# Gate and up products moved between the routing steps of a gated cross-attention and mixture-of-experts layer

## The chip, the cores and the metric

One core of a Trainium2 chip runs the whole layer in one program. The metric is the time of one execution on the device in microseconds (us), the median of several runs. The engines are PE (TensorE), DVE (VectorE), ACT (ScalarE), POOL (GpSimd) and SP (SyncE, which only issues transfers here). Each runs its own instructions in the order in which they are written, and waits on semaphores for the others.

## The reference

Inputs are x and ctx (4 batches of 512 tokens of 256 values), two gates g and the weights. All is float32.

```
x = x + tanh(g_xattn) * xattn(layernorm(x), ctx)      # 16 heads of 16, bias on q, k, v and output
h = layernorm(x)                                      # "h2" in the kernel
logits = h @ w_router;  top 2 of 8 experts, softmax over the two
moe    = sum over the two of score * (silu(h @ fc1[e][:, :256]) * (h @ fc1[e][:, 256:])) @ fc2[e]
shared = (silu(h @ gate_w) * (h @ up_w)) @ down_w     # gate_w, up_w: 256 x 512, down_w: 512 x 256
x = x + tanh(g_ffn) * (moe + shared)
```

## The kernel before

**Three stages.** First q, k, v and the attention of the 16 groups (4 batches of 4 groups of 4 heads). Last the slot stage: tokens stand sorted by expert in a DRAM tensor `slot_x`, 39 slots of 128 rows are loaded, multiplied with their expert's weights and scattered to `token_y`; behind it the shared products of batches 2 and 3 and the combination of everything. Between the two lies the stretch that the change touches, some 60 us long.

**What lies between attention and slots.** For each batch b the kernel transposes the attention's output (`ctx_transpose`), multiplies it with Wo (`out_projection`), adds it to x (`residual`, DVE), takes mean and variance (`statistics`, DVE), the reciprocal root of the variance (`rstd_second`, POOL), normalises (`normalised`, DVE), transposes (`h2_transpose`, copied out of PSUM by `h2t_first` on ACT and `h2t_second` on DVE), and multiplies with the router weights (`router`). DVE copies the logits (`logits`), picks two experts (`choose`), PE counts how many earlier tokens chose the same expert (`rank`), and DVE works out the row in `slot_x` (`place`). POOL then sends 8 indirect transfers per batch to that place (`scatter`, one per tile of 128 tokens and choice). Batches 0 to 2 have most of this behind them, or amid the last attention groups, when attention ends; batch 3 has it all ahead.

When all four batches are placed, PE sums the counts (`count`), DVE makes the table of slots (`tabulate`), SP clears the 8 ends of the experts' rows (line 355) and, when these and all 32 scatters have landed, loads the first three slots (line 362). PE transposes the first slot (`transpose_rows`, line 1321) and the slot stage begins.

**The filler.** The shared products of batches 0 and 1 need nothing but `H2T` of those batches and stand in the same stretch: `gate_up(b, c)` on PE (8 matmuls with 512 columns each), `silu(b, c)` on ACT, `hidden(b, c)` on DVE, for c from 0 to 3, then `down(b)` on PE (32 matmuls) and `shared_out(b, h)` on DVE.

**What sets the order.** It is written out by hand, once for each engine. Semaphore counts rise in that order, so the lists must fit together. PSUM has 8 banks. The routing steps take banks 3, 4 and 5 in turn, in the order of the list `USERS` (line 237), and each waits until the third step before it has been read (`bank_free`, line 1115). `gate_up` takes banks 0 and 1, or 2 and 6, or, for odd c of batch 1, banks 2 and 3; the first of these therefore waits for the logits of all batches (line 1250). It also waits until `hidden` has read the pair before the last (line 1255). `rstd_second(B - 1)` stands on POOL behind the 8 scatters of batch 0.

Of the kernel before, what the change touches and what calls it, by code (L numbers as in the profile page):

```python
# [15 lines left out]
def flamingo_layer(nc, x, ctxT, g_xattn, g_ffn, WqT, bq, WkT, bk, WvT, bv, WoT, bo,  # L16
                   w_router, fc1_w, fc2_w, gate_w, up_w, down_w, out):
    B, S, D = x.shape
# [4 lines left out]
    TB = S // P  # L23
# [5 lines left out]
    IC = ISH // P  # L29
# [26 lines left out]
    with ExitStack() as stack:  # L56
# [335 lines left out]
        def _(pool):  # L392
# [50 lines left out]
            def rstd_second(b):  # L443
                pool.wait_ge(ln_ve, B + b + 1)
                sl = slice(b * TB, (b + 1) * TB)
                nc.gpsimd.tensor_tensor(rstd[:, sl], var_eps[:, sl], minus_half[:, sl], ALU.pow).then_inc(ln_rstd, 1)  # L446

            def scatter(b):
                pool.wait_ge(tokens_in, 2)
                pool.wait_ge(placed, b + 1)  # L450
                for t in range(b * TB, (b + 1) * TB):
                    for k in range(2):
                        nc.gpsimd.indirect_dma_start(slot_x, bass.IndirectOffsetOnAxis(ap=pos[:, t, k:k + 1], axis=0),  # L453
                                                     CH[:, t, :], None).then_inc(scattered, 16)
# [5 lines left out]
            for b in range(B - 1):  # L460
                rstd_second(b)
            scatter(0)
            rstd_second(B - 1)
            for b in range(1, B):
                scatter(b)

            for j in range(SLOTS):
# [7 lines left out]
        def _(act):  # L475
# [70 lines left out]
            def ctt_first(b):  # L546
                act.wait_ge(ct_t, 2 * b + 1)
                if b >= 2:
                    act.wait_ge(wo_done, 2 * (b - 1))
                nc.scalar.copy(ctt(b, 0), PS[:, bank("ctx_t", b, 0), :]).then_inc(ctt_ready[0], 1)  # L550

            def h2t_first(b):
                act.wait_ge(h2_t, 2 * b + 1)
                nc.scalar.copy(H2T[:, 0, b * S:(b + 1) * S], PS[:, bank("h2_t", b, 0), :]).then_inc(h2t_ready[0], 1)
# [21 lines left out]
            def silu(b, c):  # L576
                n = IC * b + c
                act.wait_ge(gu_done, n + 1)
                if n >= 2:
                    act.wait_ge(hs_ready, n - 1)  # L580
                nc.scalar.activation(SG[:, n % 2, :], PS[:, gu_bank(n, 0), :], ACT.Silu).then_inc(silu_ready, 1)  # L581

            h2t_first(1)
            ctt_first(3)
            silu(0, 0)
            h2t_first(2)
            silu(0, 1)
            h2t_first(3)
            silu(0, 2)
            silu(0, 3)  # L590
            for b in range(1, BE):
                for c in range(IC):
                    silu(b, c)
                if b == 1:

                    act.wait_ge(gap_ready, 1)
                    nc.scalar.activation(sc[:, 1, :], sc[:, 0, :], ACT.Exp).then_inc(exp_sc, 1)
# [28 lines left out]
        def _(dve):  # L626
# [120 lines left out]
            def residual(b):  # L747
                dve.wait_ge(x_biased, TB * (b + 1))
                for h in range(2):
                    dve.wait_ge(wo_done, 2 * b + h + 1)  # L750
                    tt = slice(b * TB + 2 * h, b * TB + 2 * h + 2)
                    nc.vector.scalar_tensor_tensor(out=X[:, tt, :], in0=PS[:, bank("wo", b, h), :].rearrange("p (t d) -> p t d", t=2),
                                                   scalar=tg[:, 0:1], in1=X[:, tt, :], op0=ALU.mult, op1=ALU.add)\
                        .then_inc(x1_ready, 1)
# [5 lines left out]
            def h2t_second(b):  # L760
                dve.wait_ge(h2_t, 2 * b + 2)
                dve.wait_ge(st_done, G * TB * (GROUPS - 1 + b // 2))
                nc.vector.tensor_copy(H2T[:, 1, b * S:(b + 1) * S], PS[:, bank("h2_t", b, 1), :]).then_inc(h2t_ready[1], 1)

            def logits(b):
                dve.wait_ge(lg_done, b + 1)
                nc.vector.tensor_copy(LG[:, b * TB:(b + 1) * TB, :],
                                      PS[:, bank("router", b), 0:TB * E].rearrange("p (t e) -> p t e", t=TB)).then_inc(lg_ready, 1)


            def hidden(b, c):
                n = IC * b + c
                dve.wait_ge(silu_ready, n + 1)
                if b >= 2:
                    dve.wait_ge(down_done, 2 * (b - 1))
                nc.vector.tensor_tensor(HS[:, b % 2, c, :], SG[:, n % 2, :], PS[:, gu_bank(n, 1), :], ALU.mult)\  # L776
                    .then_inc(hs_ready, 1)

            def shared_out(b, h):
                dve.wait_ge(down_done, 2 * b + h + 1)  # L780
                tt = slice(b * TB + 2 * h, b * TB + 2 * h + 2)
                nc.vector.scalar_tensor_tensor(out=X[:, tt, :], in0=PS[:, 6 + h, :].rearrange("p (t d) -> p t d", t=2),
                                               scalar=tg[:, 1:2], in1=X[:, tt, :], op0=ALU.mult, op1=ALU.add)\
                    .then_inc(base_ready, 1)
# [34 lines left out]
            def place(b):  # L819
                sl = slice(b * TB, (b + 1) * TB)  # L820
                dve.wait_ge(ranked, b + 1)
                step(nc.vector.tensor_tensor(RK[:, :, :], PS[:, bank("rank", b), 0:TB * E].rearrange("p (t e) -> p t e", t=TB),
                                             ecap[:, :].unsqueeze(1).to_broadcast([P, TB, E]), ALU.add))
                step(nc.vector.tensor_tensor(PM[:, sl, :, :], OH[:, sl, :, :],
                                             RK[:, :, :].unsqueeze(2).to_broadcast([P, TB, 2, E]), ALU.mult))
                step(nc.vector.tensor_reduce(posf[:, sl, :], PM[:, sl, :, :], AX.X, ALU.add))
                nc.vector.tensor_copy(pos[:, sl, :], posf[:, sl, :]).then_inc(placed, 1)
                dve.wait_ge(placed, b + 1)
# [47 lines left out]
            def normalised(b):  # L876
                normalise(b, B, lambda t: CH[:, b * TB + t, 0:D], h2_ready)
# [20 lines left out]
            denominators(GROUPS - 1)  # L898
            head_out(GROUPS - 1)
            normalised(2)  # L900
            logits(1)
            choose(1)
            ctt_second(3)
            hidden(0, 0)
            place(1)
            residual(3)
            statistics(3)
            h2t_second(2)
            normalised(3)
            hidden(0, 1)  # L910
            logits(2)
            h2t_second(3)
            choose(2)
            hidden(0, 2)
            place(2)
            logits(3)
            choose(3)
            nc.vector.tensor_tensor(sc[:, 0, :], mx8[:, :, 1], mx8[:, :, 0], ALU.subtract).then_inc(gap_ready, 1)
            hidden(0, 3)
            place(3)  # L920
            tabulate()


            hidden(1, 0)
            for h in range(2):
                shared_out(0, h)
            for b in range(1, BE):
                for c in range(1 if b == 1 else 0, IC):
                    hidden(b, c)
                for h in range(2):  # L930
                    shared_out(b, h)

            dve.wait_ge(exp_sc, 1)
            step(nc.vector.tensor_scalar(sc[:, 2, :], sc[:, 1, :], 1.0, None, ALU.add))
# [63 lines left out]
        def _(pe):  # L998
# [164 lines left out]
            def router(b):  # L1163
                pe.wait_ge(w_in["router"], 16)
                for c in range(DC):
                    pe.wait_ge(h2t_ready[c], b + 1)
                bank_free("router", b)
                for t in range(TB):
                    for c in range(DC):
                        last = mm(PS[:, bank("router", b), t * E:(t + 1) * E], H2T[:, c, b * S + t * P:b * S + (t + 1) * P], wr[:, c, :],  # L1170
                                  start=(c == 0), stop=(c == DC - 1))
                last.then_inc(lg_done, 1)
# [63 lines left out]
            h2_transpose(1)  # L1236
            rank(0)
            out_transpose(GROUPS - 1)
            router(1)


            def gate_up(b, c):
# [33 lines left out]
            def count():  # L1276
                pe.wait_ge(placed, B)
                bank_free("count", 0)
                mm(PS[:, bank("count", 0), 0:E], ones[:, :], PRE[:, NT, :], start=True, stop=True).then_inc(counted, 1)

            ctx_transpose(3)
            gate_up(0, 0)
            rank(1)
            out_projection(3)
            h2_transpose(2)
            gate_up(0, 1)
            router(2)
            h2_transpose(3)
            gate_up(0, 2)
            rank(2)  # L1290
            router(3)
            gate_up(0, 3)
            rank(3)
            gate_up(1, 0)
            count()
            down(0)
            for b in range(1, BE):
                if b > 1:
                    gate_up(b, 0)
                for c in range(1, IC):  # L1300
                    gate_up(b, c)
                    if c == 1 and b > 1:
                        down(b - 1)


            pe.wait_ge(w_in["fc1"], 16 * DC * E // 2)
            pe.wait_ge(w_in["fc2"], 16 * (IE // P) * E // 2)
# [111 lines left out]
```

## Time and profile before

| | |
|---|---|
| median of 3 runs | 498.92 us (496.5, 498.92, 499.67) |
| the profiled execution's own time | 500.97 us |
| its span, from first to last instruction | 498.5 us |
| PE busy | 481.8 us, 97% of the span |
| DVE, ACT, POOL busy | 322.1, 224.4, 119.7 us |
| mean granted clock of PE | 0.990 of full |
| chain that ended last, PE's share | 85% |

The time of a profiled execution holds a little more than its span (2.47 us here). PE is the engine to look at; the other engines matter where PE waits for them. The granted clock is a second thing to read: a busy PE at half clock looks as busy as one at full clock.

### The profile page before, as it was taken

The numbers are of one execution on the slowest core, as the hardware profiler recorded it, in microseconds if no ns is written. First come the engines' busy times: TensorE is split into PE (matmuls) and PEld (weight loads), VectorE is DVE, ScalarE is ACT, GpSimd is POOL, SyncE is SP. The second block draws the span as 40 slices with busy tenths as digits, with TensorE's granted clock in tenths as the row PEclk, the third lists the DMA queues.
The fourth block names the chain that finished last, engine by engine and source line by source line (L and its number), as shares of the span: only waits on it lengthen the run. The fifth ranks groups of instructions, "written<-read, shape, count | busy, mean of one in ns | idle before, by whom it ended". The sixth has DMA issues, their size and how long they took to land.

```text
span 498.5 us, 7810 instructions
## 1 busy us (share of the span) xinstructions
PE 481.8 (97%) x2230; PEld 246.7 (49%) x2231; DVE 322.1 (65%) x791; ACT 224.4 (45%) x479; POOL 119.7 (24%) x136
## 2 busy tenths in 40 slices
PE   8699979999999999999999999999999999999997
PEld 8365522232323333323366666665666666665645
DVE  1868888888888888888668676333333333332574
ACT  1454357777777777777744111033322222331110
POOL 4365474000000000000000647701333333333000
PEclk9999989999999999999999799999999999999999
DMA  8479743789986222220000112612232222221831
GB/s 261 121 219 225 187 156 100 181 188 188 197 185 158 64 65 65 65 65 1 3 2 0 70 56 100 191 42 65 89 92 85 84 87 91 87 65 53 315 128 63
DMA packets 49042, 55.58 MB, mean 111 GB/s; under 512 B 7825, under 2 KB 41105, under 8 KB 49009
## 3 DMA queue, kind: packets, MB, share of 16 engines
q1 hardware_dynamic: 42864, 43.21, 33.2%
q0 software_dynamic: 3408, 9.34, 5.3%
q10 hardware_dynamic: 2736, 2.63, 1.7%
q8 instruction: 16, 0.26, 0.2%
q14 instruction: 18, 0.14, 0.1%
HBM read 35.31 MB, written 19.71 MB: 110 GB/s over the span
## 4 chain that ended last, share of the span: by engine, by line
PE 85%; DMA 5%; DVE 5%; SPq 1%; ACT 1%; issue 1%; ACTq 0%; POOL 0%; DVEq 0%
PE PS L1347 14%; PE PS L1101 11%; PE PS L1258 11%; PE PS L1033 10%; PE PS L1211 10%; PE PS L1336 7%; PE PS L1270 6%; PE PS L1083 4%; DMA R<-mparts 3%; PE PS L1059 2%; PE PS L1149 2%; DMA bias_qk<-in_bk_dram 2%; PE PS L1111 2%; PE PS L1328 2%; PE PS L1321 2%; PE PS L1170 2%
## 5 line engine op out<-in xcount | busy, mean ns | idle before, releaser
L654 DVE TENSOR_REDUCE nmax<-PS 128x1 f32<-128x512 f32 x256 | 162.3, 682 | 16.8 <-PE PS L1033 16.5
L562 ACT ACTIVATE R<-PS 128x512 f32<-128x512 f32 x256 | 133.6, 603 | 41.4 <-PE PS L1211 41.4
L1033 PE MATMUL PS<-R 96*128 96x512 bf16 x256 | 96.6, 384 | 1.7 <-DVE nmax L654 1.7
L1211 PE MATMUL PS<-R 98*128 98x512 bf16 x256 | 86.7, 382 | 2.7 <-DMA R<-mparts 1.8
L1347 PE MATMUL PS<-R 128*128 x156 | 73.6, 594 | 1.5 <-ACT R L614 1.0
L1101 PE MATMUL PS<-R 128*32 128x512 f32 x512 | 68.6, 608 | 0.0
L470 POOL DMA_INDIRECT token_y<-R,dest x39 | 37.4, 958 | 98.9 <-DVE R L944 98.6
L960 DVE TENSOR_TENSOR R<-R,PS 128x256 f32<-128x256 f32 x39 | 16.4, 421 | 68.0 <-ACT R L611 42.4
L1033 PEld LDWEIGHTS PS<-R 96*128 96x128 bf16 x256 | 24.9, 98 | 58.1 <-DVE nmax L654 41.1
L446 POOL TENSOR_TENSOR rstd<-var_eps,minus_half 128x4 f32<-128x4 f32 x4 | 4.1, 1019 | 197.2 <-DVE var_eps L637 197.2
L611 ACT ACTIVATE R<-PS 128x256 f32<-128x256 f32 x39 | 14.9, 383 | 80.3 <-PE PS L1347 80.3
L1211 PEld LDWEIGHTS PS<-R 98*128 98x128 bf16 x256 | 24.5, 98 | 41.9 <-ACT R L562 19.8
L1347 PEld LDWEIGHTS PS<-R 128*128 128x128 f32 x156 | 29.4, 190 | 22.8 <-issue 20.9
L1336 PE MATMUL PS<-fc,R 128*128 x156 | 40.0, 380 | 0.0
L581 ACT ACTIVATE R<-PS 128x512 f32<-128x512 f32 x16 | 9.6, 597 | 63.4 <-PE PS L1258 63.4
L453 POOL DMA_INDIRECT slot_x<-CH,pos x32 | 31.2, 975 | 10.6 <-issue 9.3
L1258 PE MATMUL PS<-R,wgate 128*128 128x512 f32 x64 | 32.0, 624 | 0.0
L1258 PE MATMUL PS<-R,wup 128*128 128x512 f32 x64 | 30.3, 595 | 0.0
L1270 PE MATMUL PS<-wdown,R 128*128 128x256 f32 x128 | 28.4, 380 | 0.0
L776 DVE TENSOR_TENSOR R<-R,PS 128x512 f32<-128x512 f32 x16 | 10.9, 684 | 26.3 <-ACT R L581 26.3
L1336 PEld LDWEIGHTS PS<-fc,R 128*128 128x128 f32 x156 | 26.6, 190 | 2.1
L1270 PEld LDWEIGHTS PS<-wdown,R 128*128 128x128 f32 x128 | 24.2, 190 | 4.5 <-issue 1.4
(131 smaller groups left out, 539.5 us busy)
## 6 DMA issues: line engine op xcount, KB each, us to landing
R<-q_parts SPq DMA_DIRECT2D x96, 64.0 KB, 3.2
R<-k_parts SPq DMA_DIRECT2D x96, 64.0 KB, 3.3
R<-slot_x SPq DMA_DIRECT2D x39, 129.0 KB, 2.0
R<-in_fc_w_dram SPq DMA_DIRECT2D x8, 512.0 KB, 4.2
R<-token_y SPq DMA_DIRECT2D x4, 1024.0 KB, 8.9
k_parts<-R SPq DMA_DIRECT2D x8, 384.0 KB, 3.5
q_parts<-R SPq DMA_DIRECT2D x8, 384.0 KB, 3.2
fc<-in_fc_w_dram SPq DMA_DIRECT2D x8, 256.0 KB, 5.1
```

The costliest lines, as they stand in the source:

```text
L453: nc.gpsimd.indirect_dma_start(slot_x, bass.IndirectOffsetOnAxis(ap=pos[:, t, k:k + 1], axis=0), CH[:, t, :], None).then_inc(scattered, 16)
L470: nc.gpsimd.indirect_dma_start(token_y, bass.IndirectOffsetOnAxis(ap=dest[:, j:j + 1], axis=0), YE[:, j % UN, :], None).then_inc(y_out[j % ...
L562: nc.scalar.activation(PT[:, kt, j, :], PS[:, (G * (TB * i + kt) + j) % 3, :], ACT.Exp).then_inc(exp_done, 1)
L654: nc.vector.tensor_reduce(nmax[:, i % 2, j * TB + qt:j * TB + qt + 1], PS[:, smax_bank(n), :], AX.X, ALU.max, negate=True).then_inc(max_re ...
L1033: mm(PS[:, smax_bank(n), :], QS[g][0:KS, j, qt * P:(qt + 1) * P], KST[g][0:KS, j, :], start=True, stop=True).then_inc(smax_done, 1)
L1083: last = mm(PS[:, qk_bank(b, j), :], w[:, c, (j % 2) * P:(j % 2 + 1) * P], src[:, s, c, :], start=(c == 0), stop=(c == DC - 1))
L1101: last = mm(PS[32 * j:32 * j + VW, 6, :], VA[:, b * TB + kt, (g * G + j) * VS:(g * G + j) * VS + VW], PT[:, kt, j, :], start=(kt == 0), st ...
L1211: mm(PS[:, n % 3, :], KST[g][0:KM, j, kt * P:(kt + 1) * P], QS[g][0:KM, j, :], start=True, stop=True).then_inc(st_done, 1)
L1258: last = mm(PS[:, gu_bank(n, k), :], w[:, d, c * P:(c + 1) * P], H2T[:, d, b * S:(b + 1) * S], start=(d == 0), stop=(d == DC - 1))
L1270: last = mm(PS[:, 6 + t // 2, (t % 2) * D:(t % 2 + 1) * D], HS[:, b % 2, c, t * P:(t + 1) * P], wdown[:, c, :], start=(c == 0 and t % 2 == ...
L1336: last = mm(PS[:, 5 + u, 0:D], HET[:, u, c * P:(c + 1) * P], fc2[:, c, e, :], start=(c == 0), stop=(c == IE // P - 1))
L1347: last_mm = mm(PS[:, 1 + u, :], XGT[:, u, c * P:(c + 1) * P], fc1[:, c, e, :], start=(c == 0), stop=(c == DC - 1))
```

## The change

PE begins with `gate_up(0, 0)` ahead of `router(1)` instead of behind `ctx_transpose(3)`, and from there on a pair of gate and up products stands between each two routing steps: five of batch 0 and 1 move ahead, and `gate_up(1, 1)` and `(1, 2)` stand ahead of `count`, `(1, 3)` behind `down(0)`. ACT and DVE get the matching order of `silu` and `hidden`, and DVE does `choose(2)` and `place(2)` ahead of `h2t_second(3)`. On POOL the first four scatters of batch 1 stand ahead of the root of batch 3's variance. No instruction is added or removed.

```diff
-            def scatter(b):
+            def scatter(b, tiles=(0, 1, 2, 3)):
                 pool.wait_ge(tokens_in, 2)
                 pool.wait_ge(placed, b + 1)
-                for t in range(b * TB, (b + 1) * TB):
+                for t in (b * TB + n for n in tiles):
...
             scatter(0)
+            scatter(1, (0, 1))
             rstd_second(B - 1)
-            for b in range(1, B):
+            scatter(1, (2, 3))
+            for b in range(2, B):
                 scatter(b)
...
             h2t_first(1)
+            silu(0, 0)
             ctt_first(3)
-            silu(0, 0)
+            silu(0, 1)
             h2t_first(2)
-            silu(0, 1)
-            h2t_first(3)
             silu(0, 2)
             silu(0, 3)
+            h2t_first(3)
...
             normalised(2)
+            hidden(0, 0)
             logits(1)
             choose(1)
             ctt_second(3)
-            hidden(0, 0)
             place(1)
+            hidden(0, 1)
             residual(3)
             statistics(3)
             h2t_second(2)
             normalised(3)
-            hidden(0, 1)
+            hidden(0, 2)
             logits(2)
+            choose(2)
+            hidden(0, 3)
+            place(2)
             h2t_second(3)
-            choose(2)
-            hidden(0, 2)
-            place(2)
+            hidden(1, 0)
             logits(3)
             choose(3)
             nc.vector.tensor_tensor(sc[:, 0, :], mx8[:, :, 1], mx8[:, :, 0], ALU.subtract).then_inc(gap_ready, 1)
-            hidden(0, 3)
             place(3)
+            hidden(1, 1)
             tabulate()
-            hidden(1, 0)
+            hidden(1, 2)
             for h in range(2):
                 shared_out(0, h)
-            for b in range(1, BE):
-                for c in range(1 if b == 1 else 0, IC):
-                    hidden(b, c)
-                for h in range(2):
-                    shared_out(b, h)
+            hidden(1, 3)
+            for h in range(2):
+                shared_out(1, h)
...
             out_transpose(GROUPS - 1)
-            router(1)
...
+            gate_up(0, 0)
+            router(1)
             ctx_transpose(3)
-            gate_up(0, 0)
+            gate_up(0, 1)
             rank(1)
             out_projection(3)
             h2_transpose(2)
-            gate_up(0, 1)
+            gate_up(0, 2)
             router(2)
+            gate_up(0, 3)
             h2_transpose(3)
-            gate_up(0, 2)
             rank(2)
+            gate_up(1, 0)
             router(3)
-            gate_up(0, 3)
+            gate_up(1, 1)
             rank(3)
-            gate_up(1, 0)
+            gate_up(1, 2)
             count()
             down(0)
-            for b in range(1, BE):
-                if b > 1:
-                    gate_up(b, 0)
-                for c in range(1, IC):
-                    gate_up(b, c)
-                    if c == 1 and b > 1:
-                        down(b - 1)
+            gate_up(1, 3)
```

## Rows read from the trace of the kernel before

**Rows 1.** Windows view: length, busy of PE, PEld, DVE, ACT, POOL; clock, DMA, GB/s
```profile
276.76:283.42 6.66, 6.66 (x21) 4.59 (x21) 4.96 (x27) 1.87 (x2) 5.04 (x5) 0.50 0.23 82
```

**Rows 2.** Timeline of PE, 275 to 290 us: start, length, what, [idle before]
```profile
275.66 2.55 PE L1170 MATMUL PS<-wr,R 128*128 128x8 f32 x16 [0.96 <-DVE R L763]
278.06 1.95 PE L1137 MATMUL PS<-ident,CH 128*128 128x128 f32 x8
279.80 3.62 PE L1258 MATMUL PS<-R,wgate 128*128 128x512 f32 x4
...
285.12 0.30 PE L1179 MATMUL PS<-OHS,before 128*128 128x32 f32 x2
...
285.48 3.70 PE L1149 MATMUL PS<-w_o,R 128*128 128x256 f32 x16
289.02 1.04 PE L1159 MATMUL PS<-ident,CH 128*128 128x128 f32 x8
```

**Rows 3.** Timeline of PE, 289 to 334 us
```profile
289.89 1.88 PE L1258 MATMUL PS<-R,wgate 128*128 128x512 f32 x4
...
293.33 1.85 PE L1170 MATMUL PS<-wr,R 128*128 128x8 f32 x16
295.03 1.07 PE L1159 MATMUL PS<-ident,CH 128*128 128x128 f32 x8
...
299.70 0.41 PE L1179 MATMUL PS<-OHS,before 128*128 128x32 f32 x2 [0.16 <-DVE PRE L812]
...
326.78 7.07 PE L1270 MATMUL PS<-wdown,R 128*128 128x256 f32 x32
333.69 0.38 PE L1321 MATMUL PS<-ident,R 128*128 128x128 f32 x2
```

**Rows 4.** Timeline of DVE, 287 to 314 us
```profile
287.29 0.17 DVE L827 CAST pos<-posf 128x8 uint32<-128x8 f32 x1
...
291.86 0.17 DVE L637 TENSOR_SCALAR var_eps<-mv 128x4 f32<-128x4 f32 x1
...
293.19 1.42 DVE L643 TENSOR_SCALAR CH<-X,mv,rstd 128x256 f32<-128x256 f32 x4 [0.56 <-POOL rstd L446]
294.53 0.67 DVE L776 TENSOR_TENSOR R<-R,PS 128x512 f32<-128x512 f32 x1
...
296.75 0.36 DVE L804 MAX8 mx<-LG 128x8 f32<-128x8 f32 x4
...
298.87 0.77 DVE L812 TENSOR_TENSOR PRE<-PRE,OHS 128x8 f32<-128x8 f32 x4
...
302.20 0.19 DVE L767 COPY LG<-PS 128x32 f32<-128x32 f32 x1 [0.42 <-PE PS L1170]
...
309.74 0.29 DVE L833 TENSOR_TENSOR cnt_gt<-PS,io 128x128 f32<-128x128 f32 x1 [1.93 <-PE PS L1279]
...
313.44 0.17 DVE L852 TENSOR_SCALAR eid<-eidf 1x39 int32<-1x39 f32 x1
```

**Rows 5.** Timeline of POOL, 277 to 324 us
```profile
277.15 1.20 POOL L453 DMA_INDIRECT slot_x<-CH,pos  x1 [1.26 <-DVE pos L827]
...
286.24 0.96 POOL L453 DMA_INDIRECT slot_x<-CH,pos  x1 [0.30 <-issue]
292.11 1.04 POOL L446 TENSOR_TENSOR rstd<-var_eps,minus_half 128x4 f32<-128x4 f32 x1 [4.91 <-DVE var_eps L637]
...
322.70 0.96 POOL L453 DMA_INDIRECT slot_x<-CH,pos  x1 [0.30 <-issue]
```

**Rows 6.** Timeline of SP's queue, 312 to 340 us
```profile
314.34 6.90 SPq L355 DMA_DIRECT2D slot_x<-ZERO  x8
325.50 1.45 SPq L362 DMA_DIRECT2D R<-slot_x  x3
```

**Rows 7.** Source view of line 355: how long its eight transfers took
```profile
DMA to landing us min/median/max: 2.4/3.6/3.8
```

**Rows 8.** Source view of line 362: how long its three loads took
```profile
DMA to landing us min/median/max: 2.0/2.2/2.2
```

More of the change, by code:

```diff
@@ L1279, in count @@
                 mm(PS[:, bank("count", 0), 0:E], ones[:, :], PRE[:, NT, :], start=True, stop=True).then_inc(counted, 1)
+            assert BE == 2 and IC == 4
+            gate_up(0, 0)
+            router(1)
             ctx_transpose(3)
-            gate_up(0, 0)
+            gate_up(0, 1)
             rank(1)
```

## The prediction

> **What bounds the kernel now.** I read the page first: PE is busy for 97% of the span and holds 85% of the chain that ended last, so a microsecond saved on another engine counts only where PE waits for it. Then I went through the stretch from the end of attention to the first slot in the timeline of PE, and asked for the granted clock in short windows. Two things cost time there that is not work. PE stands idle for 0.96 us ahead of `router(1)`, waiting for DVE's copy of batch 1 (L763), and for 0.16 us ahead of `rank(2)` [rows 2, 3]. And from 276.76 to 283.42 the granted clock is 0.50, the level of 1.2 GHz, with PE busy all the time [rows 1]; before and behind it is 1.00. What PE did just before the fall: transposes, two products of 32 columns, the idle time, and half of `router(1)`, whose matmuls have 8 columns. The page's section of shares calls this stretch fully busy; only the clock shows the loss. At half clock 6.66 us hold 3.33 us of work. As a check, the eight transposes of `ctx_transpose(3)` take 278.06 to 279.80, 1.74 us, where eight of `h2_transpose(2)` at full clock take 289.02 to 289.89, 0.87 [rows 2, 3].
>
> Everything from the first slot on is one chain on PE with fixed steps, so what the stretch gains up to `transpose_rows(0, 0)`, at 333.69 [rows 3], I pass on to the end undiminished.
>
> **The sum on PE.** PE is free at 275.66 - 0.96 = 274.70 and reaches the first slot at 333.69 [rows 2, 3]: 58.99 us, made of 0.96 + 0.16 of waiting, 3.33 for the clock, and 54.54 of work at full clock. No matmul is added or removed, so the 54.54 stay.
>
> The new order puts `gate_up(0, 0)` at 274.70. It needs batch 0's `H2T` and the last exponentials, both there well before, so the 0.96 us are filled; and matmuls of 512 columns stand where idle time and 8-column matmuls stood. I take the clock's 3.33 us as won in full. Its ends are 0 and 3.33; the row that decides is that the later groups of the same small products, `router(2)` with eight transposes from 293.33 on, stood between gate and up products and the clock stayed at 1.00.
>
> Then I walk the list, each step from start to start: `gate_up` 3.44 (289.89 to 293.33), `router` 1.70 (293.33 to 295.03), `ctx_transpose` and `h2_transpose` 0.87, `rank` 0.36 (285.12 to 285.48), `out_projection` 3.54 (285.48 to 289.02), `down` 6.91 (326.78 to 333.69) [rows 2, 3].
> `gate_up(0,0)` ends at 278.14, `router(1)` 279.84, `ctx_transpose(3)` 280.71, `gate_up(0,1)` 284.15, `rank(1)` 284.51, `out_projection(3)` 288.05, `h2_transpose(2)` 288.92, `gate_up(0,2)` 292.36, `router(2)` 294.06, `gate_up(0,3)` 297.50, `h2_transpose(3)` 298.37. Up to here I find no wait: `choose(1)` takes 2.89 us (296.75 to 299.64, as `choose(2)`) [rows 4] and fits beside `gate_up(0,1)`.
>
> **Waits that are new.** (1) `rank(2)`. `out_projection(3)` ended at 289.02 and batch 3's variance was ready 3.01 us later, at 292.03 [rows 2, 4]; now 288.05 + 3.01 = 291.06. The root stands behind four scatters more. The last of batch 0 ends at 287.20 and one takes 0.96 + 0.30 = 1.26 [rows 5], so four more end at about 292.3, the root starts at 292.45 instead of 292.11, and `normalised(3)` at 293.54 instead of 293.19 [rows 4, 5]: earlier statistics, a root 0.35 us later. Behind it DVE does 1.42 of normalising, `hidden(0,2)` 0.67, the logits 0.19, `choose(2)` 2.89 [rows 4]: 298.75, against PE at 298.37. With the semaphore's way PE waits 0.4 us. Ends: 0, and 0.96 as the longest wait for DVE in the rows.
> (2) `gate_up(1,1)` writes bank 3 and so waits for the logits of batch 3, from a router that ends right before it. The product's tail is 1.85 - 1.70 = 0.15 us [rows 3], the copy 0.19 [rows 4], with two semaphore hops about 0.42. DVE is free then (`hidden(1,0)` is done about 303.9, `router(3)` ends at 304.5). Ends 0.3 and 0.96.
> `rank(3)` comes after `choose(3)` (2.89 us, beside a `gate_up` of 3.44): no wait. `hidden` and `silu` for the two-ahead rule always have a product of 3.44 us to hide in.
> So PE needs 54.54 + 0.4 + 0.42 = 55.36 us and reaches the first slot at 330.06, 3.63 us sooner.
>
> **Is the slot there by then?** Two things must land. The scatters: `place(1)` is done 2.34 us behind the start of `rank(1)` (285.12 to 287.46, and that held a `hidden`) [rows 2, 4]; now by 284.15 + 2.34 = 286.5, before POOL is free at 287.20, so POOL never stops there. Batch 2 is placed by about 301.2, and 16 scatters at 1.26 start the last at 320.1 instead of 322.70 [rows 5]. It cost nothing on PE before and is now 2.6 us earlier. The clearing: `count` moves behind two more products. Counted back from the first slot, behind it lie two `down` and, before, three `gate_up` (24.14 us: 309.55), now one (17.26 us: 312.80), so it is 3.25 us later. Table, clearing and landing follow at their own pace: eight clearings from 314.34 over 6.90 us become 317.6 to 324.5 [rows 6]. The last starts at about 324.1 and takes 2.4 to 3.6 us (2.4 was the shortest, and now no scatter runs beside the last) [rows 7]: 326.5 to 327.7. The first load takes 2.2 [rows 8]: the slot is there at 328.8 to 330.0. The load was issued at 325.50 before, held by the last scatter [rows 6]. So PE's 330.06 and the transfers' 330.0 nearly meet. I put 0.1 us for it; ends 0 and 1.2.
> ACT's and DVE's reordering by itself costs nothing: it lies beside products of 3.44 us. If that cover went, a `hidden` of 0.67 us is the price of each.
>
> **Sum:** 3.63 - 0.1, a gain of 3.5 us. Against the profiled execution's own time that is 500.97 - 3.5 = 497.5; the median of the runs stands 2.05 us below that execution, and 498.92 - 3.5 = **495.4 us**.
>
> **Rivals.** (A) The clock falls all the same. The change leaves small products and two waits of 0.4 us in the stretch, one with the eight transposes of `h2_transpose(3)` and `rank(2)` around it. For it: the fall before came behind a wait of just 0.96 us. Against it: the 0.16 us wait amid small products at 299.70 [rows 3] brought no fall. Then the 3.33 are lost again, the gain is 0.2, and the time 498.7. The Trainium skill speaks for this rival (TensorE: Matmul & The Clock Gate, "A second HAM failure mode: psum-queue depth-cycling"): a PE that is idle for short moments between groups of matmuls while it cycles PSUM banks can swing between its two levels. By that rule the two new waits count against the change and the sum would be rival A's.
> (B) The change's first part works, but the clearing of `slot_x` becomes the bound: `count` comes late, the transfers meet other traffic, and PE waits 1 to 2 us at line 1321. For it: the 0.06 us of slack above. Against it: I took the long end of the landing. Gain 2: 497.
> (C) Slower: the root behind the scatters. If batch 1 is placed late, the four scatters start late and the root of batch 3 with them. It decides from 287.20 on; every microsecond beyond is one more of PE waiting at `rank(2)`. In the worst case the scatters start just before the variance is ready at 291.06: the root starts at 296.1, 3.65 us later than reckoned, PE idles for 4 us and the clock falls as it did before, 3.33 more. 3.5 - 3.65 - 3.33 = -3.5, so 502.4. Against it: batch 1 is placed 0.7 us ahead of that point, by a bound on the long side.
>
> **How the numbers follow.** A measurement of this kernel tells about 1%, 5.0 us, from no change. My forecast (gain 2.5 to 4.6, the latter with no new wait: 0.96 + 0.16 + 3.33, and a little) has 0.73, A 0.15, B 0.07, C 0.05. The runs before spread from 496.5 to 499.67, so a median can lie some 1 us off either way. The range goes down to 495.4 - 1.0 - 1.0 = 493.4 and up to take in most of A, 498.6. Faster by over 1% means below 493.9. That needs the forecast's upper end and a lucky median: 0.19. Slower by over 1% means above 503.9, only beyond C: 0.03. Within 1%: 0.78.
>
> **What the new profile would show.** Clock 1.00 at 275 to 285 us and no wait of PE before `router(1)`. PE waits of about 0.4 us at L1179 (third) and at the first L1258 behind the last L1170. The root of batch 3 (L446) at 292.4, with four L453 ahead of it. The last L453 near 320, L362 near 327. L1321 first at 330.1. A stretch at 0.50 anywhere in 275 to 340 would show A, an idle PE ahead of L1321 B, a late fourth L446 C.

## The result, and the profile after

| | before | changed |
|---|---|---|
| median of 20 runs, us | 499.19 (495.6 to 504.06) | 497.19 (495.26 to 499.03) |
| ratio | | 0.9954, 95% interval 0.9938 to 0.9969 |
| profiled execution: span, us | 498.5 | 494.8 |
| mean granted clock in it | 0.990 | 0.997 |
| first slot's transposes start | 333.69 | 329.94 |

The kernel is 0.46% faster, 2.3 us (1.5 to 3.1); the ratio is taken over all the runs, here and below, and is not the quotient of the two medians. The forecast was a gain of 3.5 us and a median of 495.4 us, with a range from 493.4 to 498.6 that holds the measured 497.19.

The windows view of the changed kernel (length, busy of PE, PEld, DVE, ACT, POOL; clock, DMA, GB/s): up to `gate_up(0, 0)`, from there to the first slot, the slots, the rest.
```profile
262.00:274.87 12.87, 12.87 (x93) 9.00 (x86) 10.39 (x46) 6.25 (x13) 1.01 (x1) 1.00 0.00 0
274.87:329.94 55.07, 54.66 (x232) 36.83 (x231) 32.34 (x135) 8.74 (x14) 33.22 (x34) 1.00 0.30 104
329.94:446.00 116.06, 114.52 (x451) 71.55 (x450) 44.55 (x159) 36.50 (x115) 33.41 (x35) 1.00 0.26 81
446.00:494.80 48.80, 45.46 (x147) 27.11 (x145) 24.03 (x48) 5.70 (x11) 3.82 (x4) 1.00 0.40 140
```
The same two stretches behind it in the kernel before:
```profile
333.69:449.70 116.01, 114.47 (x451) 71.54 (x450) 44.53 (x159) 36.48 (x115) 33.55 (x35) 1.00 0.27 81
449.70:498.50 48.80, 45.50 (x147) 27.10 (x145) 24.03 (x48) 5.70 (x11) 3.83 (x4) 1.00 0.39 140
```
What follows the first slot is as long as before, within 0.05 us. The stretch had 58.99 us with the clock at 0.50 for 6.66 of them [rows 1 to 3]; now it has 55.07 at 1.00. Counted from the same product in both, the last `out_transpose` (L1111, 274.06 before and 274.40 after), the stretch takes 59.63 us before and 55.54 after, 4.09 less:
```profile
274.06 0.64 PE L1111 MATMUL PS<-ident,R 128*128 128x128 f32 x4
```

Timeline of PE, changed kernel (start, length, what, [idle before]):
```profile
274.40 0.64 PE L1111 MATMUL PS<-ident,R 128*128 128x128 f32 x4
274.87 1.88 PE L1257 MATMUL PS<-R,wgate 128*128 128x512 f32 x4
...
278.31 1.85 PE L1170 MATMUL PS<-wr,R 128*128 128x8 f32 x16
280.01 1.07 PE L1137 MATMUL PS<-ident,CH 128*128 128x128 f32 x8
...
297.78 1.04 PE L1159 MATMUL PS<-ident,CH 128*128 128x128 f32 x8
298.94 0.41 PE L1179 MATMUL PS<-OHS,before 128*128 128x32 f32 x2
...
302.93 1.85 PE L1170 MATMUL PS<-wr,R 128*128 128x8 f32 x16
305.06 1.98 PE L1257 MATMUL PS<-R,wgate 128*128 128x512 f32 x4 [0.28 <-DVE LG L769]
...
323.04 7.07 PE L1269 MATMUL PS<-wdown,R 128*128 128x256 f32 x32
329.94 0.38 PE L1317 MATMUL PS<-ident,R 128*128 128x128 f32 x2
```
No wait ahead of `router(1)`, which takes 1.70 us instead of 2.40 [rows 2]. The two new waits are there. Eight transposes take 0.87 us, so `rank(2)` could start at 298.65 and starts at 298.94: 0.29 us. `gate_up(1, 1)` could start at 302.93 + 1.70 = 304.63 and starts at 305.06: 0.43.

POOL and the queue of SP, changed kernel:
```profile
286.58 0.96 POOL L453 DMA_INDIRECT slot_x<-CH,pos  x1 [0.30 <-issue]
...
291.64 0.96 POOL L453 DMA_INDIRECT slot_x<-CH,pos  x1 [0.30 <-issue]
292.62 1.04 POOL L446 TENSOR_TENSOR rstd<-var_eps,minus_half 128x4 f32<-128x4 f32 x1
...
320.29 0.96 POOL L453 DMA_INDIRECT slot_x<-CH,pos  x1 [0.30 <-issue]
```
```profile
317.40 6.94 SPq L355 DMA_DIRECT2D slot_x<-ZERO  x8
326.55 1.45 SPq L362 DMA_DIRECT2D R<-slot_x  x3
```
Batch 1's scatters follow batch 0's without a pause; the root stands behind four of them, at 292.62 instead of 292.11, though its input was ready sooner [rows 5]. The last scatter starts 2.4 us sooner, the clearing 3.06 later, the loads 1.05 later [rows 6]; the first load lands about 328.6, 1.3 us ahead of PE.

### The profile page after: what moved, and what is told of

Read it like the earlier page. It is cut to its first block, busy times and chain, and to the rows that moved or that the text cites. A ratio compares the mean times of both kernels' runs of the same rounds, so it can differ in the third digit from the quotient of the medians.

```text
span 494.8 us, 7811 instructions
## 1 busy us (share of the span) xinstructions
PE 478.3 (97%) x2230; PEld 245.6 (50%) x2231; DVE 322.3 (65%) x791; ACT 224.4 (45%) x479; POOL 119.5 (24%) x136
## 4 chain that ended last, share of the span: by engine, by line
PE 81%; DVE 5%; DMA 5%; POOL 3%; issue 2%; SPq 2%; ACT 1%; ACTq 1%; DVEq 0%; POOLq 0%
PE PS L1343 14%; PE PS L1101 11%; PE PS L1033 10%; PE PS L1211 10%; PE PS L1257 8%; PE PS L1332 7%; PE PS L1269 6%; PE PS L1083 4%; DMA R<-mparts 2%; PE PS L1059 2%; POOL slot_x L453 2%; PE PS L1111 2%; DMA bias_qk<-in_bk_dram 2%; PE PS L1324 2%; PE PS L1317 2%
## 5 line engine op out<-in xcount | busy, mean ns | idle before, releaser
L656 DVE TENSOR_REDUCE nmax<-PS 128x1 f32<-128x512 f32 x256 | 162.1, 681 | 16.5 <-PE PS L1033 15.9
L1257 PE MATMUL PS<-R,wgate 128*128 128x512 f32 x64 | 30.4, 598 | 0.3 <-DVE LG L769 0.3
L1101 PEld LDWEIGHTS PS<-R 128*32 128x32 f32 x512 | 10.1, 108 | 26.8 <-ACT R L564 24.1
```

The source lines that it names most:

```text
L656: nc.vector.tensor_reduce(nmax[:, i % 2, j * TB + qt:j * TB + qt + 1], PS[:, smax_bank(n), :], AX.X, ALU.max, negate=True).then_inc(max_re ...
L1101: last = mm(PS[32 * j:32 * j + VW, 6, :], VA[:, b * TB + kt, (g * G + j) * VS:(g * G + j) * VS + VW], PT[:, kt, j, :], start=(kt == 0), st ...
L1257: last = mm(PS[:, gu_bank(n, k), :], w[:, d, c * P:(c + 1) * P], H2T[:, d, b * S:(b + 1) * S], start=(d == 0), stop=(d == DC - 1))
```

## The experiments

All are one job's kernels against runs of the kernel before on the same chip. Beside each ratio stands the **clock loss**: (1 - mean granted clock) x span, the mean over the timed executions; "the rest" is the span without it. It counts every stretch at half clock, wherever in the program, also where PE is not the bound, so it is not time lost one for one. Over the 63 timed executions of the kernel before in the second and third job, one more microsecond of clock loss goes with 0.08 us (give or take 0.12) of longer span. A difference of two such means is uncertain by 1.3 to 1.7 us (95%). The three jobs ran on three chips.

**First job, a disturbed chip.** The kernel before took 508.0 us there. In the first profile's stretch no wait is marked "remote". Here ACT and DVE stood while the scatters ran. Waits view from 275 to 330 us of the kernel before on this chip (who waited for what: us in total, times, longest), then of the kernel with POOL's part alone:
```profile
ACT R L581 <- remote: 14.0, 2, 11.0
...
DVE LG L767 <- remote: 2.9, 1, 2.9
DVE RK L822 <- remote: 2.2, 1, 2.2
```
```profile
ACT R L583 <- remote: 22.4, 2, 13.1
...
DVE X L784 <- remote: 9.0, 1, 9.0
...
DVE R L765 <- remote: 2.2, 1, 2.2
```
Behind "remote" the profile names no instruction that released the wait. PE in turn waits up to 4.87 us at once in these profiles (filler, for `place(3)` ahead of `count`). So the ratios of this job say more of those stalls than of the edits, and three of the four kernels were run again later.

*The kernel before, again* (no edit). 

> The kernel before once more, nothing changed, for more executions of it with their granted clock. Open is why the measured gain (ratio 0.9954, about 2.3 us) is smaller than the 3.5 us of the sum, although the profiled stretch gained what was reckoned. Theory T1: the fall of the clock between attention and slots, worth 3.33 us, comes in only some executions of the kernel before, about half to two thirds of them. Then the profile of this run shows it or not, the mean clock differs between its executions in steps of about 0.0067 (6.66 us at half clock in 498), and the times scatter by 3 us. Theory T2: the fall comes in every execution of the kernel before, and the changed kernel has a fall of its own in some. Then the profile shows the fall at 276 us again, and the ratio to the kernel before is 1.00 in both theories.


Ratio 0.9999 (0.9970 to 1.0027). The clock loss is 8.65 us in both. The profile shows a fall near 276 us, but a short one (rows below), and a second one from 292.9 to 296.3 us, 2 us behind the start of `router(2)`, for which PE had waited 0.41 us.

*The first move alone.*
```diff
             out_transpose(GROUPS - 1)
-            router(1)
...
-            ctx_transpose(3)
             gate_up(0, 0)
+            router(1)
+            ctx_transpose(3)
             rank(1)
```


> The kernel before with one move on PE: gate_up(0, 0) ahead of router(1) instead of behind ctx_transpose(3). If the filled wait and the clock are the whole gain, this gets all of it: 0.96 us of waiting gone and no stretch at half clock from 276 to 283 us, so 2.3 us (T1, fall in some executions) up to 4.3 us (T2, fall in all), ratio 0.991 to 0.9955. The rival that the rest of the reordering matters expects less than half of the gain here, ratio 0.998 or more.


Ratio 1.0041 (1.0014 to 1.0068): slower. The first theory is out; the rival's bound (0.998 or more) holds, but nothing foresaw a loss. Taken up in the third job.

*Filler.*
```diff
             out_transpose(GROUPS - 1)
+            pe.wait_ge(w_in["shared"], 48)
+            pe.wait_ge(exp_done, G * TB * GROUPS)
+            mm(PS[:, 0, :], ones[:, :], wgate[:, 0, :], start=True, stop=True)
             router(1)
```


> The kernel before with one more product of 512 columns (two matmul instructions, 0.86 us, its result is overwritten) on PE ahead of router(1), where PE waited 0.96 us; nothing is reordered. If the idle time is what lets the clock fall, the clock stays at 1.00 here and the gain is the clock's part alone: 1.5 us (T1) to 3.3 us (T2), ratio 0.993 to 0.997. If the fall comes from the small products around it and not from the idle time, the clock falls as before and the ratio is 1.000.


Ratio 0.9976 (0.9943 to 1.0009); clock loss 7.32 us against 8.65. Not decided by the time, nor by the clock loss (1.33 us less, give or take 1.4). The clock from 274 to 286 us is 1.00 (row below), but it falls at 300.2 and 313.9 us.

*POOL's part alone.* The edit is the first two blocks of the change. 

> The kernel before with the POOL part of the change alone: four scatters of batch 1 ahead of the root of batch 3. Batch 1 is placed at 287.5 us, so the four end about 292.5 and the root comes 0.4 us later than before; normalised(3) feeds h2_transpose(3) and, by h2t_second(3) and choose(2), rank(2), where PE waited 0.16 us: that wait grows to about 0.5 us. The scatters end some 4 us sooner and PE does not wait for them in either. All theories: 0.3 to 0.4 us slower, ratio 1.000 to 1.001; PE reaches the first slot 0.3 us later.


Ratio 1.0094 (1.0060 to 1.0128), 4.8 us slower where 0.3 was expected, of which 3.2 (give or take 1.5) lie in the rest of the span (497.0 to 500.1). The root came at 293.03, on time as reckoned; the profile shows instead the stalls above, one of them DVE's copy of batch 2 ahead of `router(2)`, where PE waits 1.99 us. It was not run on a quiet chip; the next job has the opposite edit on one.

**Second job, a quiet chip** (kernel before 499.88 us, clock loss 5.51, the rest 491.96).

*The changed kernel, again.* 

> The changed kernel once more, unchanged, beside the kernel before on the chip of this job. Open since the repeat of the kernel before: on its chip DVE and ACT stood for 2 to 15 us in the stretch of the scatters with their operands long there (marked remote or issue), and the kernel took 508 us instead of 499. If the chip is a quiet one, as that of the first two profiles: ratio 0.995, first slot at 330 us. If it is a disturbed one: theory T3, that such stalls hit any order of the stretch alike and cost by how much PE must wait for DVE there. The new order lets PE wait for DVE at rank(2), gate_up(1, 1) and count as the old one does, but puts five products more between: ratio 0.990 to 1.000, and PE waits of over 1 us at L1179, L1257 or L1278 in the profile.


Ratio 0.9956 (0.9937 to 0.9975), the first result repeated. The span is 2.5 us shorter (give or take 0.9): clock loss 3.84 us, 1.67 less; the rest 491.13, 0.83 less. Neither share is clear of noise by itself (1.7 and 1.5 either way). Over the 31 executions of this job that have the new order on PE up to `down(1)` (this run, the root first, the first slot amid `down(1)`), the clock loss is 1.9 us less (give or take 1.1), which is clear of noise.

*The root first.*
```diff
             scatter(0)
-            scatter(1, (0, 1))
             rstd_second(B - 1)
-            scatter(1, (2, 3))
+            scatter(1)
```


> The changed kernel with POOL's old order: the root of batch 3 ahead of all scatters of batch 1. By the sum the root then comes at 291.2 instead of 292.6, choose(2) ends 1.4 us sooner, and the wait of PE at rank(2) (0.13 us more than a rank without wait in the profile of the changed kernel) is gone; the scatters of batch 1 begin 2.3 us later but batch 2's still wait for place(2). So 0.1 to 0.2 us faster than the changed kernel, not measurable, on a quiet chip. If the root's place matters more (rival: with POOL's part alone the kernel before became 0.9% slower), this is 1 us or more faster than the changed kernel.


Ratio 0.9950 (0.9933 to 0.9967), the rest 491.37. POOL's part is worth nothing that the times can show on this chip, in either direction. The profile shows its price: with the root first, `rank(2)` starts 0.87 us behind the eight transposes (298.75 to 299.62), so the 0.29 us wait is gone, and the stretch is 0.38 us shorter (table below).

*The first product back.*
```diff
-            gate_up(0, 0)
             router(1)
             ctx_transpose(3)
+            gate_up(0, 0)
             gate_up(0, 1)
```
with `silu(0, 0)` and `hidden(0, 0)` at their old places. 

> The changed kernel with gate_up(0, 0) back behind router(1) and ctx_transpose(3), and silu(0, 0) and hidden(0, 0) at their old places. If the first move is the gain: PE waits 0.96 us ahead of router(1) again, the clock falls to 0.50 near 276 us in most executions, and the kernel is 2 to 4 us slower than the changed one, about as the kernel before. If the rest of the order carries the gain, it stays within 1 us of the changed kernel.


Ratio 1.0009 (0.9988 to 1.0030), clock loss 5.51, the rest 491.83. The gain is gone, all of it. PE waits 0.96 us ahead of L1170 again, and the clock falls from 277.2 to 280.6 us, a short fall:
```profile
273.02 0.63 PE L1111 MATMUL PS<-ident,R 128*128 128x128 f32 x4
274.61 1.92 PE L1170 MATMUL PS<-wr,R 128*128 128x8 f32 x16 [0.96 <-DVE R L765]
...
331.06 0.38 PE L1317 MATMUL PS<-ident,R 128*128 128x128 f32 x2
```
Without the first move the rest of the order brings nothing.

*The first slot amid down(1).*
```diff
+                        if between is not None and c == IC - 1 and t == 2:
+                            between()
...
-            down(BE - 1)
-            transpose_rows(0, 0)
+            down(BE - 1, lambda: transpose_rows(0, 0))
```


> The changed kernel, and PE transposes the first slot amid the last products of down(1) (ahead of the last 4 of its 16 products) instead of behind them, so that ACT's copy (0.37 us) hides the 0.55 us that PE waits there. The slot's rows land about 328.8 us, and the transposes would now stand at about 329.1. Expected gain 0.3 to 0.5 us on a quiet chip, if the transfers stay in time; 0 if they are the bound (rival B of the prediction), with the wait then ahead of L1317.


Ratio 0.9943 (0.9920 to 0.9966), from 7 runs. Its difference from the changed kernel is inside both intervals.

**Third job, a quiet chip** (kernel before 499.52 us, clock loss 5.80, the rest 491.31).

*The first move alone, again.* 

> The kernel before with gate_up(0, 0) ahead of router(1) on PE alone, again, since the first run of it fell on a chip where ACT and DVE stood for up to 16 us amid the scatters. On a quiet chip (kernel before at about 499.5): the idle 0.96 us and the half clock go, and rank(1), which now comes 3.4 us behind router(1) instead of 5.3, waits about 1 us more for choose(1). By what the last job showed of the clock (granted clock short of full by 5.5 us of span in the kernel before, 3.8 in the changed one), the gain is 1.7 + 0.96 - 1 = 1.7 us, ratio 0.9965, with a mean clock 0.0035 above the kernel before. Rival, that the products between the other routing steps matter too: ratio 0.999 to 1.001. On a disturbed chip: slower, as the first time.


Ratio 1.0054 (1.0034 to 1.0074): 2.7 us slower, with the clock loss up by 1.54 us and the rest by 1.40, each with an uncertainty about as large as itself. In its profile the stretch is 2.89 us longer than in the kernel before (table below). The expectation named the wait ahead of `rank(1)`, but had it at 1 us and the kernel faster; the rival's 0.999 to 1.001 missed too. Timeline of PE:
```profile
280.45 1.07 PE L1137 MATMUL PS<-ident,CH 128*128 128x128 f32 x8
283.72 0.64 PE L1179 MATMUL PS<-OHS,before 128*128 128x32 f32 x2 [2.19 <-DVE PRE L812]
284.17 0.61 PE L1180 MATMUL PS<-PRE,ones 128*128 128x32 f32 x2
284.64 6.51 PE L1149 MATMUL PS<-w_o,R 128*128 128x256 f32 x16
...
301.67 0.41 PE L1179 MATMUL PS<-OHS,before 128*128 128x32 f32 x2 [0.16 <-DVE PRE L812]
301.92 0.39 PE L1180 MATMUL PS<-PRE,ones 128*128 128x32 f32 x2
302.14 1.93 PE L1170 MATMUL PS<-wr,R 128*128 128x8 f32 x16
303.93 3.66 PE L1257 MATMUL PS<-R,wgate 128*128 128x512 f32 x4
```
`gate_up(0, 0)` covered `choose(1)` where it stood. Moved ahead alone, it leaves `rank(1)` waiting 2.19 us, and the clock falls behind that wait instead: `out_projection(3)` takes 6.35 us from start to start instead of 3.54 [rows 2]. The change put `gate_up(0, 1)` there. A second, short fall comes from 304.0 to 307.4 us, 2.3 us behind the 0.16 us wait ahead of `rank(2)`: the gate product at 303.93 takes 3.49 us from start to start. The kernel before has the same wait and the same small products there, and no fall in its first profile [rows 3].

*Filler, again.* 

> The kernel before with one unused product of 512 columns in PE's idle time ahead of router(1), again. On a quiet chip: if the idle time lets the clock fall, the mean clock rises by 0.0035 and the time falls by 1.7 us, ratio 0.9965; the idle time itself is not won, since useless work fills it. If the small products around it are the cause, ratio 1.000 and the same mean clock as the kernel before. On the disturbed chip the ratio was 0.9976 with an interval that held 1.


Ratio 0.9991 (0.9972 to 1.0009), clock loss 5.05, that is 0.75 less (give or take 1.25). The forecast of the clock theory, 0.9965, lies just outside the interval; its rival's 1.000 lies inside. So the time speaks against a gain as large as 1.7 us, while the profiles speak for the clock theory. The windows view from 274 to 286 us, one row a kernel, in this order. First the five that have the 0.96 us of idle time: the kernel before in its first profile, on the disturbed chip, and in the third job, the changed kernel with the first product back, and the kernel before with POOL's part alone.
```profile
274.00:286.00 12.00, 11.04 (x45) 7.71 (x45) 7.53 (x40) 2.51 (x4) 7.97 (x8) 0.72 0.19 67
```
```profile
274.00:286.00 12.00, 11.63 (x52) 9.06 (x53) 8.57 (x39) 2.47 (x3) 8.54 (x9) 0.86 0.22 78
```
```profile
274.00:286.00 12.00, 11.04 (x48) 7.80 (x47) 8.04 (x41) 2.60 (x5) 7.51 (x8) 0.72 0.18 64
```
```profile
274.00:286.00 12.00, 11.39 (x42) 6.54 (x43) 7.19 (x34) 2.47 (x3) 8.61 (x9) 0.86 0.22 78
```
```profile
274.00:286.00 12.00, 10.98 (x64) 8.44 (x63) 10.40 (x47) 3.26 (x5) 7.28 (x8) 1.00 0.16 56
```
Then the two with filler (disturbed chip, third job), and the changed kernel in its two profiles.
```profile
274.00:286.00 12.00, 11.85 (x64) 8.69 (x63) 10.11 (x47) 2.98 (x4) 7.56 (x8) 1.00 0.19 66
```
```profile
274.00:286.00 12.00, 11.85 (x70) 8.06 (x70) 10.78 (x48) 3.61 (x5) 6.11 (x7) 1.00 0.12 44
```
```profile
274.00:286.00 12.00, 12.00 (x60) 8.04 (x59) 9.55 (x46) 3.45 (x5) 7.69 (x8) 1.00 0.19 67
```
```profile
274.00:286.00 12.00, 12.00 (x56) 7.94 (x55) 9.33 (x43) 2.59 (x4) 8.27 (x9) 1.00 0.19 70
```
In the fifth row the clock falls later, at 293.2 us, behind the 1.99 us wait ahead of `router(2)`. With the idle time the clock falls here four times in five; with useless work in its place and the same small products around it (twice), or with `gate_up(0, 0)` there (the five profiles of the new order), it never does. And the fall has two sizes: 0.72 over 12 us is a loss of 3.4 us, 0.86 one of 1.7. The mean over the five is 2.0.

The length of the stretch tells what a fall costs. From the start of the last `out_transpose` to the first slot's transposes, profiles of the quiet chips:

| kernel | stretch, us | clock's loss in it | at full clock |
|---|---|---|---|
| before, first profile and third job | 59.63, 59.63 | 3.41, 3.41 | 56.22 |
| changed, the first product back | 58.04 | 1.71 | 56.33 |
| before with filler | 56.49 | 0 | 56.49 |
| changed, and again | 55.54, 55.53 | 0 | 55.5 |
| changed, the root first | 55.16 | 0 | 55.16 |
| first move alone | 62.52 | 3.41 + 1.71 | 57.40 |

Two ends of the stretch, of the kernel before in the third job and with filler:
```profile
274.58 0.64 PE L1111 MATMUL PS<-ident,R 128*128 128x128 f32 x4
...
334.21 0.38 PE L1321 MATMUL PS<-ident,R 128*128 128x128 f32 x2
```
```profile
276.28 0.63 PE L1111 MATMUL PS<-ident,R 128*128 128x128 f32 x4
...
332.77 0.38 PE L1324 MATMUL PS<-ident,R 128*128 128x128 f32 x2
```
In this stretch a fall costs its loss one for one, and the filler itself costs 0.27 us. If it prevents falls worth 0.7 us in the mean, its measured gain of 0.45 us (from 1.4 faster to 0.4 slower) comes out; up to 1.7 us is inside the interval. The falls in the first 80 us are another matter. The ten profiles of the quiet chips lose from 0 to 5.1 us there, and PE comes to the last `out_transpose` at 274.35 and 274.84 in the two without a fall and at 273.02 and 276.28 in the two with the most: no delay can be seen.

*Both level edits together.* The root first, and the first slot amid `down(1)`. 

> The changed kernel with both edits that came out level or a little ahead of it: the root of batch 3 ahead of the scatters of batch 1, and the first slot's transposes amid the last products of down(1). Alone they gave 0.9950 and 0.9943 against 0.9956 for the changed kernel, all within each other's intervals. Together: the 0.55 us wait ahead of the first L1343 gone, the wait at rank(2) 0.1 us shorter: ratio 0.994 to 0.995 to the kernel before. If the first slot's transfers are the bound (rival B), no better than 0.9956.


Ratio 0.9960 (0.9942 to 0.9979). The wait ahead of the first slot's product is gone in the profile:
```profile
328.73 0.44 PE L1318 MATMUL PS<-ident,R 128*128 128x128 f32 x2
329.01 1.03 PE L1270 MATMUL PS<-wdown,R 128*128 128x256 f32 x4
329.87 1.88 PE L1344 MATMUL PS<-R 128*128 x4
```
and that product starts 55.52 us behind the last `out_transpose`, against 56.47 in the changed kernel. The times don't show these 0.95 us: no version here is measurably ahead of the changed kernel.

*The kernel before, a third time.* 

> The kernel before, unchanged, for one more look at its clock. The three profiles so far that kept router(1) behind the idle time show a fall there each time, but of different length: 6.66 us in the first, 3.4 us in the repeat and 3.4 us in the changed kernel with gate_up(0, 0) back. Theory T1b: the fall comes nearly always and is 3.4 us or 6.7 us long, so the first profile showed a long one; this profile shows a fall at 275 to 284 us of one of the two lengths. T1 (no fall in a good part of the executions): it may show none. Ratio 1.000.


Ratio 1.0006 (0.9984 to 1.0028); the long fall, 0.72 (third row above). T1b and T1 are both partly right: the fall comes in most executions, not in all, and in two lengths.

## Why the prediction was right, point by point

**Direction, place and range: right.** The gain lies where the sum put it, and 497.19 us is inside the range. PE reached the first slot at 329.94 (forecast 330.06), the root came at 292.62 (292.45), the waits were 0.29 and 0.43 us (0.4 and 0.42), the clearing began at 317.40 (317.6), the loads at 326.55 (near 327), the last scatter at 320.29 (320.1). Part of this close match is luck: the changed kernel's profile reached the last `out_transpose` 0.34 us later than the one before. Counted from there, PE took 55.54 us to the first slot, where the walk gives 330.06 - 274.06 = 56.00. (By its own steps the walk has `router(3)` end at 304.3, not 304.5; nothing else rests on that.)

**The idle time: slightly too small.** I took 0.96 us as all that the first move fills. After `out_transpose` PE goes on 0.47 us behind its start (274.40 to 274.87), not 0.64: the shown length holds a tail that the next product overlaps. So 1.13 us were filled, and at full clock the stretch is 56.22 - 55.54 = 0.68 us shorter where the sum had 0.2 to 0.3. (The rest of the span in the timed executions says 0.83, give or take 1.5.)

**The clock: the term that was mis-sized.** I took the fall of the one profile, 3.33 us (3.41 in windows of 0.1 us, from 276.75 to 283.58), as what every execution loses. The five profiles with the idle time show two long falls of 3.4 us, two short ones of 1.7 and one with none, 2.0 in the mean. What the clock is worth on average can be had in two ways. The measured gain of 2.3 us less the 0.68 at full clock leaves 1.6 (0.8 to 2.4); the filler on the quiet chip leaves 0.7 (-0.2 to 1.7). Both allow 0.8 to 1.7, so the clock is between a third and three quarters of the gain, and its exact share stays open. The difference of clock loss in the 42 timed executions of the second job, 1.67 us (give or take 1.7), agrees and doesn't narrow it. The first profile was a long draw. (The clock also falls in the first 80 us, in 12 of the 14 profiles; that scatters the clock loss of single executions.)

**Rival A** (the clock falls all the same) did not come: 1.00 from 274 to 340 us in all five profiles that have PE's new order. All five hold the 0.43 us wait ahead of `gate_up(1, 1)`, three of them the 0.29 us wait ahead of `rank(2)`. But the evidence against A was weaker than it looked. I leaned on one profile in which the old order's `rank(2)`, behind a wait of 0.16 us, and `router(3)` brought no fall. Six profiles have this wait in this order, and in three of them the clock falls 2.2 to 3.1 us behind its end (the first move alone twice, the filler on the disturbed chip). The new order puts `gate_up(1, 0)` between these two steps; whether that is why it has no fall there is not shown. The section of the Trainium skill that spoke for A (TensorE: Matmul & The Clock Gate, "A second HAM failure mode: psum-queue depth-cycling") is not borne out for the two new waits. That the clock falls behind short idle moments the traces do show: behind 0.96 us in four of five profiles, and behind 2.19 us in both of the first move alone.
**Rival B** (the clearing as the bound): not here, the first slot landed 1.3 us ahead. No clearing took more than 3.2 us in this profile, where I had reckoned with up to 3.6. In the four other profiles of the new order the longest took 3.6 to 4.1, and with the root first the first load, issued at 328.08 and 2.1 us long, landed only 0.3 us ahead of PE (330.52). So B is close.
**Rival C** (the root behind the scatters): batch 1 was placed in time. The root behind the scatters cost the 0.29 us wait at `rank(2)` that the sum had, and swapping the two back moved nothing that the times show on a quiet chip. On the disturbed one POOL's part alone cost 4.8 us, with the root on time, so by another way than C's.

**What I had not seen.** The sum called "54.54 us of work" unchanged and walked the list once. That walk was right, but it didn't show that the moves hold each other up: `gate_up(0, 0)` alone makes the kernel 0.54% slower, all but it makes no difference, together they give 0.46%.

**Left open.** Why the filler gained less time than the falls in the profiles suggest. What ACT and DVE wait for on the disturbed chip while the scatters run, and why the old PE order with POOL's new one lost most. No run took scatters away there, and the changed kernel was not timed on it.

## What to carry to other kernels

Look at the granted clock beside the busy share: here about a microsecond of idle time amid small products was followed in four of five profiles by a fall that cost 1.7 or 3.4 us, more than the idle time itself. A loss at low clock read from one profile is one draw, and so is its absence; look at several profiles before putting a number on it, and compare the length of the stretch between two fixed products. The mean clock of all executions times the span also counts falls that cost nothing, so only its difference between two kernels says something, and it is noisy. Before a product is moved ahead to fill a hole, ask which later wait it covered, and move the next one into its place.

## What the runs showed of the hardware

- The clock's loss near 276 us is 0, 1.7 or 3.4 us with the same PE order, and 0 in all seven profiles without idle time ahead of `router(1)` or `rank(1)`.
- A fall in this stretch lengthens it by its loss (59.63 us with the long one, 58.04 with the short one, 56.49 with filler and none). Falls in the first 80 us, up to 5.1 us of loss, don't show in when the stretch begins.
- Three of six profiles with a wait of 0.16 us ahead of `rank(2)` and `router(3)` right behind it have a fall there. That the wait is the cause is not shown.
- The kernel before took 499.5 and 499.9 us on two chips and 508.0 on a third. There the clock loss was 8.65 us instead of 5.5 to 5.8, and ACT stood for up to 11.0 us at once in the stretch of the scatters (15.9 with the first move alone), waiting for nothing that the profile names.
